# First turns and last turns of a gated linear-attention layer: W_out's high part by ScalarE, the scale-and-shift table in another PSUM bank, early z and h of the last group but one, and a residual added by TensorE

## The chip, the core and the metric

The kernel runs on one core of one Trainium2 chip. The metric is the time of one execution on the device in microseconds (us), the median of several. The engines are TensorE (PE in the profile; its weight loads are PEld), VectorE (DVE), ScalarE (ACT), GpSimd (POOL) and SyncE (SP), which here issues DMAs only. Each engine works through its own list of instructions in order and waits on semaphores that the others raise. SBUF is the working memory, PSUM the eight banks of 2 KB per partition into which TensorE writes; GpSimd cannot reach PSUM in this kernel's code, the others can.

## What is computed

`x` has 128 sequences of 64 rows of 256 numbers, in float32:

```python
xn = ln(x) * ln_w + ln_b
q = softmax((xn @ Wq + bq) in 8 heads of 32, over the 32)
k = softmax((xn @ Wk + bk - 1e6 * (1 - mask)) in 8 heads, over the 64 rows)
v = (xn @ Wv + bv) * mask
att = k^T v                      # per sequence and head, 32 x 32
y = q att                        # per sequence and head
scale, shift = split(silu(cond) @ W_emb + b_emb)
h = silu((ln(y) * ln2_w + ln2_b) * (1 + scale) + shift)
out = x + h @ W_out + b_out
```

Products are carried to near float32 accuracy as three products of rounded parts: with a = a_hi + a_lo and w = w_hi + w_lo, TensorE adds a_hi w_hi + a_hi w_lo + a_lo w_hi.

## The kernel before

The 8192 rows are cut into 16 groups of 512 rows (8 sequences, four tiles of 128 rows). A body function per engine, `body(i, ...)`, is one turn. Turns -1, 0, 1 and 2 are written out, turns 3 to 12 are a hardware loop of two turns per pass (on TensorE up to 14), the last turns are written out, and `tail()` ends each engine's list. The software pipeline has three stages: turn i does k, q and v of group i, attention and y of group i - 1, and layer norm of y, z, h and the output product of group i - 2. The last group, 15 (`L`), is worked in halves in the tail; group 14 is `M`. The order of each engine is the order of the code; nothing is scheduled by a tool.

For every group, x is brought in twice, as rows (`x_all`) and transposed (`xt_raw`). VectorE takes mean and variance per row (`x_stats`: `xstat`, `xmv`), GpSimd turns them into a scale and an offset per row (`x_rstd`: four small instructions on `xr`), VectorE turns these into rows (`x_rows`), SyncE writes them to DRAM with four small DMAs (`rows_stored`) and reads them back spread over all partitions (`rows_loaded`), and GpSimd applies them to `xt_raw` in four passes (`x_scaled`). ScalarE rounds the result to `xt_hi` (`x_high`), VectorE subtracts for `xt_lo` (`x_low`). `x_stats(g)` waits until `x_rstd(g - 1)` is done, since `xmv` has one buffer. Groups 0 and 1 go another way: their normed rows `xhat` are made directly, by ScalarE and GpSimd, and TensorE transposes them.

In turn i VectorE masks k and takes its maxima (`k_masked`, `k_max`), ScalarE takes exp(k) and copies it back after TensorE has transposed it (`exp_k_copied`), VectorE subtracts q's maxima (`q_max`, `q_shifted`), ScalarE takes exp(q), and after q's transposes it copies them (`q_copied`). `attention` and `y_product` on TensorE follow, with `kv_scaled` on VectorE between them. `y_sums` and `y_scaled_all` bring y out of PSUM, which frees the four banks `by`; `y_stats`, `y_scale` and `y_hat_all` are the second layer norm. In turn 0, VectorE's maxima of k have their own path: GpSimd subtracts them (`k_shifted`).

The banks: `by` is four banks. All four hold y between `y_product` and `y_scaled_all`. `be` names the first two, also used for the transposes of exp(k) and for attention; `bt` names the other two, also used for the transposes of q and for tanh(z). `bk` and `bv` are two banks each, for k, q and v and the output.

Three things are done once in turn 1: W_out is halved and split into `w_o_hi` and `w_o_lo` (`weights_o`, VectorE, lines 861 to 865), the condition's silu is finished (`silu_cond`), and TensorE makes the table of scale and shift (`emb_products`, line 1141) after the last q,v tile. It writes into bank `be[1]`, for which it waits until y of group 0 has been read, `ys_d`. ScalarE copies the table (`emb_copied`), and TensorE's second half of exp(k)'s transposes waits for that copy, because it writes the same bank.

In the tail TensorE adds residuals with an identity product: `x_added` starts the accumulation in the output's bank with x (plus bias, added by GpSimd in `x_biased`), and the output product goes on top. The result is then only copied. Groups up to 13 are added by VectorE (`residual`, line 1006) instead. The tail's `half_...` functions treat the two halves of group 15. SyncE stores group 14 when both halves' results of it are in `x_all`, and then group 15 in three pieces.

## Time and profile before

| | us |
|---|---|
| median of 3 runs | 306.88 (306.3 to 309.34) |
| the profiled execution's own time | 307.7 |
| its span, first to last instruction | 305.8 |
| TensorE busy | 291.8 (95%) |
| VectorE busy | 272.4 (89%) |
| GpSimd busy | 244.6 (80%) |
| ScalarE busy | 237.0 (77%) |

The granted clock of TensorE is 1.0 of full speed over the whole span. Matmuls overlap in the pipeline, and their ends are modelled, so what counts on TensorE is the start of one against the start of the next and the idle time that the profile names. In a timeline a row is: start, length, engine, line, operation, what it writes and reads, how many instructions are merged in it, and in brackets how long the engine stood idle before it and which instruction released it. Neighbouring instructions overlap by some 0.1 us, so a row's end lies a little behind the next row's start.

### The profile page before, as it was taken

What the parts mean: (1) busy time and instruction counts of PE and PEld (TensorE: products, weight loads), DVE (VectorE), ACT (ScalarE), POOL (GpSimd) and SP (SyncE); (2) the same over time, 40 slices, a digit from 0 to 9 for tenths busy, and PEclk for the clock granted to TensorE, in tenths of its full rate; (3) what the DMA queues carried; (4) which work ended last, traced back from release to release, by engine and by line L of the source; (5) the groups of instructions that cost most, each with busy time, mean ns of one, the idle gap of its engine ahead of it and who ended that gap; (6) DMA issues with size and microseconds to landing.
All of it is one profiled execution on the core that took longest, in us unless ns stands there. A gap on an engine that the chain in (4) does not pass through costs nothing.

```text
span 305.8 us, 14375 instructions
## 1 busy us (share of the span) xinstructions
PE 291.8 (95%) x5528; PEld 248.5 (81%) x5528; DVE 272.4 (89%) x640; ACT 237.0 (77%) x592; POOL 244.6 (80%) x246
## 2 busy tenths in 40 slices
PE   7999789899999999999999999999999999989875
PEld 7578588788989888988889898889888898877655
DVE  5899999989999999999999999999999796967793
ACT  1567758787978988898979888888989798776443
POOL 2275748989998989999998989898999979873470
PEclk9999999999999999999999999999999999999999
DMA  6983430704527080815325180906251341002024
GB/s 198 315 298 109 129 115 5 236 10 117 198 66 248 1 308 1 253 56 176 133 106 203 46 263 1 298 11 231 78 169 71 90 150 53 17 4 72 4 71 137
DMA packets 28445, 38.61 MB, mean 126 GB/s; under 512 B 2433, under 2 KB 20481, under 8 KB 28418
## 3 DMA queue, kind: packets, MB, share of 16 engines
q1 hardware_dynamic: 28000, 37.94, 38.1%
q8 instruction: 17, 0.28, 0.4%
q10 hardware_dynamic: 418, 0.30, 0.3%
q14 instruction: 10, 0.08, 0.1%
HBM read 29.80 MB, written 8.45 MB: 125 GB/s over the span
## 4 chain that ended last, share of the span: by engine, by line
PE 82%; DVE 9%; issue 4%; POOL 2%; DMA 1%; POOLq 1%; ACT 0%; SPq 0%; DVEq 0%
PE bk L1113 27%; PE bv L1113 27%; PE by L1113 15%; PE by L1198 4%; PE by L1177 4%; PE bv L1189 4%; DVE xstat L785 2%; DMA x_all<-in_x 1%; DVE k_t L909 1%; DVE q_s L898 1%; POOLq L45 1%; DVE qmax L890 1%; DVE th L843 1%; POOL xr L485 1%; DVE ystat L986 0%
## 5 line engine op out<-in xcount | busy, mean ns | idle before, releaser
L641 ACT ACTIVATE k_t<-k_t,kmax 128x64 f32<-128x64 f32 x240 | 60.5, 336 | 6.4 <-DVE kmax L916 6.2
L476 POOL TENSOR_TENSOR x_all<-x_all,bo_all 128x1024 f32 (+1 forms) x16 | 40.1, 2508 | 0.2
L436 POOL TENSOR_TENSOR h_lo<-h_s,h_hi 128x512 fp32r<-128x512 f32 x30 | 38.3, 1297 | 0.9 <-ACT h_hi L660 0.8
L445 POOL TENSOR_TENSOR xt_raw<-xt_raw,rows 128x512 f32<-128x512 f32 x28 | 37.0, 1322 | 1.5 <-DMA rows<-rows_dram 1.5
L447 POOL TENSOR_TENSOR xt_raw<-xt_raw,rows 128x512 f32<-128x512 f32 x28 | 36.5, 1303 | 2.2
L286 POOL TENSOR_TENSOR z_s<-z_s,mod_shift 128x512 f32<-128x512 f32 x30 | 30.7, 1044 | 6.8 <-DVE z_s L930 6.8
L595 ACT ACTIVATE y_s<-y_s,yr 128x256 f32<-128x256 f32 x56 | 29.1, 593 | 3.8 <-POOL yr L468 3.8
L1113 PE MATMUL bv<-w_o_hi,h_hi 128*128 128x256 f32 x120 | 31.6, 285 | 0.0
L1113 PE MATMUL bv<-w_o_lo,h_hi 128*128 128x256 f32 x120 | 31.0, 280 | 0.0
L580 ACT ACTIVATE v_s<-bk,small 128x256 f32<-128x256 f32 x32 | 15.1, 474 | 17.7 <-PE bk L1113 16.4
L1113 PEld LDWEIGHTS by<-kv,q_t 32*64 32x64 f32 x2048 | 22.4, 130 | 6.9 <-issue 6.5
L466 POOL TENSOR_TENSOR yr<-yr,neg_half 128x4 f32<-128x4 f32 x15 | 15.3, 1017 | 14.9 <-DVE yr L994 14.9
L1113 PE MATMUL bk<-xt_hi,w_k_hi 128*128 128x512 f32 x64 | 26.6, 416 | 0.3 <-ACT xt_hi L603 0.3
L580 ACT ACTIVATE v_s<-bv,small 128x256 f32<-128x256 f32 x32 | 15.2, 474 | 13.4 <-PE bv L1113 13.0
L1113 PE MATMUL bk<-xt_hi,w_k_lo 128*128 128x512 f32 x64 | 25.3, 395 | 0.0
L1113 PE MATMUL by<-kv,q_t 32*64 32x33 f32 x2048 | 24.4, 226 | 1.0 <-issue 1.0
L1113 PE MATMUL bv<-w_o_hi,h_lo 128*128 128x256 f32 x120 | 24.1, 282 | 0.2 <-POOL h_lo L436 0.2
L909 DVE SCALAR_TENSOR_TENSOR k_t<-off,bk 128x512 f32<-128x512 f32 x32 | 21.8, 680 | 2.1 <-PE bk L1113 1.7
L1113 PEld LDWEIGHTS bv<-w_o_hi,h_hi 128*128 128x128 f32 x120 | 22.6, 188 | 0.9 <-issue 0.2
L1113 PEld LDWEIGHTS bv<-w_o_lo,h_hi 128*128 128x128 f32 x120 | 22.6, 188 | 0.8 <-issue 0.2
L916 DVE TENSOR_REDUCE kmax<-k_t 128x8 f32<-128x512 f32 x32 | 21.8, 681 | 1.5
L454 POOL TENSOR_SCALAR xr<-xmv 128x4 f32<-128x4 f32 x15 | 14.3, 952 | 11.1 <-DVE xmv L789 9.9
(163 smaller groups left out, 865.9 us busy)
## 6 DMA issues: line engine op xcount, KB each, us to landing
x_all<-in_x SPq DMA_DIRECT2D x15, 512.0 KB, 6.4
out<-x_all SPq DMA_DIRECT2D x15, 512.0 KB, 5.0
xt_raw<-in_x_t SPq DMA_DIRECT2D x14, 512.0 KB, 6.1
rows<-rows_dram SPq DMA_DIRECT2D x14, 512.0 KB, 4.2
off<-in_mask_rows SPq DMA_DIRECT2D x16, 256.0 KB, 6.1
rows_dram<-xr_rows SPq DMA_DIRECT2D x56, 1.0 KB
x_all<-in_x SPq DMA_DIRECT2D x2, 256.0 KB, 3.5
z_s<-in_w_emb SPq DMA_DIRECT2D x1, 512.0 KB, 7.2
```

The costliest lines, as they stand in the source:

```text
L286: return eng.tensor_tensor(z, z, mod_shift[:, c, span(g, GB)].unsqueeze(2).broadcast_to([P, GB, SEQ]), ALU.add)
L436: nc.gpsimd.tensor_tensor(h_lo[:, c, :], h_s[:, c, :], h_hi[:, c, :].bitcast(fp32), ALU.subtract).then_inc(hlo_d, 1)
L445: nc.gpsimd.tensor_tensor(xc, xc, rows[:, parity, 0, :], ALU.mult).then_inc(xm_d, 1)
L447: nc.gpsimd.tensor_tensor(xc, xc, rows[:, parity, 1, :], ALU.add).then_inc(xs_d, 1)
L466: nc.gpsimd.tensor_tensor(yr[:, 1, :], yr[:, 0, :], neg_half[:, :], ALU.pow).then_inc(yr_d, 1)
L476: nc.gpsimd.tensor_tensor(xg, xg, bo_all[:, :].unsqueeze(1).broadcast_to([P, T, D]), ALU.add).then_inc(xb_d, 1)
L580: nc.scalar.activation(v_s[:, par, t, :, 0:DH], bqv[t][:, D:2 * D].rearrange("p (h d) -> p h d", d=DH), ACT.Copy, scale=mask_c[:, i * T + ...
L595: nc.scalar.activation(y_s[:, t, :], y_s[:, t, :], ACT.Identity, scale=yr[:, 1, t:t + 1], bias=yr[:, 3, t:t + 1]).then_inc(yhat_d, 1)
L641: last = nc.scalar.activation(kk, kk, ACT.Exp, scale=-1.0, bias=kmax[:, c, n:n + 1])
L909: nc.vector.scalar_tensor_tensor(k_t[:, par, c, :], off[:, par, :], sign, bk_[c][:, :], ALU.mult, op).then_inc(kadd_d, 1)
L916: nc.vector.tensor_reduce(out=kmax[:, c, :], in_=k_t[:, par, c, :].rearrange("p (b s) -> p b s", s=SEQ), axis=AX.X, op=ALU.max if first(i) ...
L1113: return nc.tensor.matmul(dst, lhsT, rhs, start=start, stop=stop)
```

## The change

The change has two parts.

**First two turns.** W_out is no longer halved in place. ScalarE writes the rounded half of it, `w_o_hi`, in turn 0, with scale 0.5 in the copy, between the first and the second v tile; VectorE makes `w_o_lo` in turn 1 in one instruction, 0.5 W_out - w_o_hi. Two of the four `xhat` tiles of group 1 go from ScalarE to GpSimd. In turn 0, VectorE takes q's maxima and differences ahead of and in the middle of the statistics of group 2; `x_rows(2)` goes from before `x_low(1)` to the end of the turn. GpSimd adds the bias to group 0's rows before `x_rstd(2)` instead of after it. In turn 1, VectorE scales y of group 0 before it shifts q of group 1. The table of scale and shift goes to bank `bt[1]`, the fourth of `by`, and the wait for its copy goes from the transposes of exp(k) to the second half of the transposes of q.

**End.** z of group 14 is scaled before the residual of group 13, and the first half of h of group 14 is made before y of group 15 is read. Its high and low parts get buffers of their own: the tiles of `w_qv_hi` and `w_qv_lo`, free after the last q,v tile. ScalarE makes the two high parts apart, GpSimd the two low parts apart, the first of them before the last group's `y_rstd`. The residual of group 13's second half is no longer added by VectorE: TensorE starts that bank with an identity product, and ScalarE copies the result. TensorE takes `x_added` of group 14's second half ahead of the last transposes of y.

```diff
+        h_hi_m = w_qv_hi
+        h_lo_m = w_qv_lo
...
@@ GpSimd, body, turn -1
                     x_rstd(1)
+                    pool.wait_ge(xt_d, 2)
+                    pool.wait_ge(xr_d, 8)
+                    for t in (2, 3):
+                        nc.gpsimd.tensor_scalar(xhat[:, t, :], x_all[:, 1, t * D:t * D + D], xr[:, 0, t:t + 1],
+                                                xr[:, 1, t:t + 1], ALU.mult, ALU.add).then_inc(xhat_d, 1)
...
@@ GpSimd, body
                 if first(i):
                     k_shifted(0)
                     k_shifted(1)
+                    x_biased(0)
                     x_rstd(2)
...
@@ GpSimd, end
+            def late_low(c):
+
+                pool.wait_ge(hhi_d, 2 * M + c + 1)
+                nc.gpsimd.tensor_tensor(h_lo_m[:, c, :], h_s[:, c, :], h_hi_m[:, c, :].bitcast(fp32),
+                                        ALU.subtract).then_inc(hlo_d, 1)
+
             def tail():
                 shifts(M)
+                late_low(0)
                 y_rstd(0)
                 y_half_hat(0)
                 y_rstd(1)
                 y_half_hat(1)
-                h_low(M, 0)
-                h_low(M, 1)
+                late_low(1)
...
@@ ScalarE
+            def weights_o_high():
+
+                act.wait_ge(wo_in, 16)
+                nc.scalar.activation(w_o_hi[:, :, :], w_o, ACT.Copy, scale=0.5).then_inc(wo_high, 1)
...
-                for t in range(T):
+                for t in (0, 1):
                     nc.scalar.activation(xhat[:, t, :], x_all[:, 1, t * D:t * D + D], ACT.Identity,
...
-                    nc.scalar.activation(emb[:, j, :], be[1][:, j * BATCH:(j + 1) * BATCH], ACT.Identity,
+                    nc.scalar.activation(emb[:, j, :], bt[1][:, j * BATCH:(j + 1) * BATCH], ACT.Identity,
...
                     v_tile(0, 0, 0)
+                    weights_o_high()
                     v_tile(0, 0, 1)
                     x_hat_one()
+                    v_tile(0, 0, 2)
                     k_exp_first(0)
-                    v_tile(0, 0, 2)
                     v_tile(0, 0, 3)
...
+            def late_high(c):
+
+                act.wait_ge(qv_d, 4 * L + 4)
+                act.wait_ge(h_d, 2 * M + c + 1)
+                nc.scalar.activation(h_hi_m[:, c, :], h_s[:, c, :], ACT.Copy).then_inc(hhi_d, 1)
...
                 z_tanh(M, th_of)
+                late_high(0)
+                result_out(L - 2, 1, bv_, o_d, 2 * (L - 2) + 2, res_d)
                 act.wait_ge(yr_d, 2 * L + 2)
                 y_hat(0)
-                h_high(M, 0)
-                h_high(M, 1)
+                late_high(1)
...
@@ VectorE
-            def weights_o():
-
-                dve.wait_ge(wo_in, 16)
-                link(nc.vector.tensor_scalar(w_o, w_o, 0.5, None, ALU.mult))
-                split(w_o, w_o_hi, w_o_lo)
+            def weights_o_low():
+
+                dve.wait_ge(wo_high, 1)
+                nc.vector.scalar_tensor_tensor(w_o_lo[:, :, :], w_o, 0.5, w_o_hi[:, :, :].bitcast(fp32),
+                                               ALU.mult, ALU.subtract).then_inc(weights_ready, 1)
...
                 if first(i):
-                    x_stats(2, 0)
-                elif not (isinstance(i, int) and i + 2 >= G):
+                    q_max(0, 0)
+                    q_shifted(0, 0, 0)
+                    x_variances(2, 0, (0, 1, 2))
+                    q_max(0, 1)
+                    q_shifted(0, 0, 1)
+                    x_variances(2, 0, (3,))
+                    x_means(2)
+                    x_low(1, by[:, 2:4, :])
+                    x_stats(3, 1)
+                    x_rows(2)
+                    return
+                if not (isinstance(i, int) and i + 2 >= G):
                     x_rows(i + 2)
...
-                if B:
-                    y_sums(i - 1)
-                q_shifted(i, par, 0)
-                if B:
+                y_sums(i - 1)
+                if second(i):
+                    y_scaled_all(0)
+                    q_shifted(1, 1, 0)
+                else:
+                    q_shifted(i, par, 0)
                     y_scaled_all(i - 1)
...
             def tail():
                 kv_scaled(L)
+                z_scaled(M)
                 residual(L - 2, 0)
-                z_scaled(M)
+                h_product(M, 0, th_of)
                 y_sums(L)
...
-                h_product(M, 0, th_of)
                 h_product(M, 1, th_of)
                 half_z(0)
-                residual(L - 2, 1)
                 half_z(1)
...
@@ TensorE
-                        last = mm(be[1][:, j * BATCH:(j + 1) * BATCH], w_e[c // 2][:, c % 2, j * P:(j + 1) * P],
+                        last = mm(bt[1][:, j * BATCH:(j + 1) * BATCH], w_e[c // 2][:, c % 2, j * P:(j + 1) * P],
...
                 for e in range(2):
-                    if second(g) and e == 1:
-                        pe.wait_ge(emb_out, 2 * C)
                     wait(pe, ys_d, 2 * (g - 1) + 2)
...
                 for c in range(C):
                     wait(pe, ys_d, 2 * g)
+                    if second(g) and c == 1:
+                        pe.wait_ge(emb_out, 2 * C)
...
                 pe.wait_ge(qsub_d, 4 * L + 2)
-                out_product(L - 2, 1)
                 pe.wait_ge(xb_d, G)
+                x_added(L - 2, 1, bv_)
+                out_tiles(bv_[1], h_hi, h_lo, 1, None, False).then_inc(o_d, 1)
...
-                pe.wait_ge(res_d, 2 * (L - 2) + 1)
+                pe.wait_ge(res_d, 2 * (L - 2) + 2)
                 x_added(M, 0, bv_)
+                x_added(M, 1, bv_)
                 half_y_transposed(1)
-                pe.wait_ge(res_d, 2 * (L - 2) + 2)
-                x_added(M, 1, bv_)
-                out_product(M, 0)
-                out_product(M, 1)
+                late_out(0)
+                late_out(1)
```

Three places show the order in the lists. A row is the line, the operation, what it writes and reads, and the semaphores that it waits for. First, VectorE in turn 0 from the end of k's maxima (`kmax`) to the first mask of turn 1; `xstat` and `xmv` are the statistics, `xt_lo` is group 1's low part, `xr_rows` is `x_rows`. Before:

```order
L916 TENSOR_REDUCE kmax<-k_t 128x8 [waits kadd_d]
L785 BN_STATS xstat<-x_all 128x6 [waits xr_d,x_in0]
L785 BN_STATS xstat<-x_all 128x6 x3
L789 BN_AGGR xmv<-xstat 128x2 [waits xstat_d] x4
L890 TENSOR_REDUCE qmax<-bv 128x16 [waits v_d]
L898 TENSOR_TENSOR q_s<-bv,qmax 128x512 [waits qmax_d]
L890 TENSOR_REDUCE qmax<-bk 128x16 [waits v_d]
L898 TENSOR_TENSOR q_s<-bk,qmax 128x512 [waits qmax_d]
L795 STREAM_TRANSPOSE xr_rows<-xr 128x32 [waits xr_d]
L923 TENSOR_TENSOR xt_lo<-by,xt_hi 128x1024 [waits hi_d]
L785 BN_STATS xstat<-x_all 128x6 [waits xr_d,x_in1]
```

And in the changed kernel:

```order
L926 TENSOR_REDUCE qmax<-bv 128x16 [waits v_d]
L934 TENSOR_TENSOR q_s<-bv,qmax 128x512 [waits qmax_d]
L818 BN_STATS xstat<-x_all 128x6 [waits xr_d,x_in0]
L818 BN_STATS xstat<-x_all 128x6 x2
L926 TENSOR_REDUCE qmax<-bk 128x16 [waits v_d]
L934 TENSOR_TENSOR q_s<-bk,qmax 128x512 [waits qmax_d]
L818 BN_STATS xstat<-x_all 128x6 [waits xr_d,x_in0]
L825 BN_AGGR xmv<-xstat 128x2 [waits xstat_d] x4
L959 TENSOR_TENSOR xt_lo<-by,xt_hi 128x1024 [waits hi_d]
L818 BN_STATS xstat<-x_all 128x6 [waits xr_d,x_in1]
L818 BN_STATS xstat<-x_all 128x6 x3
L831 STREAM_TRANSPOSE xr_rows<-xr 128x32 [waits xr_d]
```

The means of group 2 now come after q, and `xr_rows` has moved behind the statistics of group 3, which wait for `xr_d` of group 2.

Second, GpSimd in turn 0, from the end of `x_rstd(1)`; `k_t` is `k_shifted`, `x_all` is `x_biased(0)`, and the four `xr` rows after it are `x_rstd(2)`. Before:

```order
L425 TENSOR_TENSOR k_t<-k_t,kmax 128x512 [waits kmax_d] x2
L454 TENSOR_SCALAR xr<-xmv 128x4 [waits xmv_d,xhat_d]
L456 TENSOR_TENSOR xr<-xr,neg_half 128x4 [waits xr_d]
L458 TENSOR_TENSOR xr<-xmv,xr 128x4 [waits xr_d]
L460 TENSOR_SCALAR xr<-xr 128x4 [waits xr_d]
L476 TENSOR_TENSOR x_all<-x_all,bo_all 128x1024 [waits xstat_d,xhat_d,bo_in]
```

And in the changed kernel:

```order
L497 TENSOR_SCALAR xhat<-x_all,xr 128x256 [waits xr_d,xt_d]
L497 TENSOR_SCALAR xhat<-x_all,xr 128x256
L428 TENSOR_TENSOR k_t<-k_t,kmax 128x512 [waits kmax_d] x2
L479 TENSOR_TENSOR x_all<-x_all,bo_all 128x1024 [waits xstat_d,xhat_d,bo_in]
L457 TENSOR_SCALAR xr<-xmv 128x4 [waits xmv_d,xhat_d]
L459 TENSOR_TENSOR xr<-xr,neg_half 128x4 [waits xr_d]
L461 TENSOR_TENSOR xr<-xmv,xr 128x4 [waits xr_d]
L463 TENSOR_SCALAR xr<-xr 128x4 [waits xr_d]
```

Two `xhat` tiles stand ahead of `k_shifted`, and `x_biased(0)` stands ahead of `x_rstd(2)`.

Third, VectorE in the tail, from `kv_scaled` of group 15 to the first statistics of its y; `z_s` is z of group 14, `h_s` its h, `rq` is `y_sums`. Before:

```order
L947 TENSOR_TENSOR kv<-by,rk 128x4x66
L1006 TENSOR_TENSOR x_all<-bv,x_all 128x512 [waits o_d,xb_d]
L930 TENSOR_TENSOR z_s<-bk,mod_scale 128x512 [waits h_d,yt_d] x2
L966 RECIPROCAL rq<-by 128x32 [waits yr_d,y_d,ys_d,yt_d]
L977 TENSOR_TENSOR y_s<-by,rq 128x512 [waits rq_d]
```

And in the changed kernel:

```order
L983 TENSOR_TENSOR kv<-by,rk 128x4x66
L966 TENSOR_TENSOR z_s<-bk,mod_scale 128x512 [waits h_d,yt_d] x2
L1042 TENSOR_TENSOR x_all<-bv,x_all 128x512 [waits o_d,xb_d]
L991 SCALAR_TENSOR_TENSOR h_s<-th,z_s 128x512 [waits hlo_d,th_d]
L1002 RECIPROCAL rq<-by 128x32 [waits yr_d,y_d,ys_d,yt_d]
L1013 TENSOR_TENSOR y_s<-by,rq 128x512 [waits rq_d]
```

The residual has changed places with z, and one product of h stands ahead of `y_sums`.

## Rows read from the trace of the kernel before

**Rows 1.** Stretch of the loop: length, busy time (instructions) per engine, clock, DMA share, GB/s.

```profile
60.70:263.38 202.68, 202.68 (x4082) 176.15 (x4081) 187.69 (x439) 174.41 (x444) 186.45 (x175) 1.00 0.39 127
```

**Rows 2.** Timeline of TensorE in turns 1 and 2: start, length, instruction [idle <-releaser].

```profile
31.66 1.49 PE L1113 MATMUL by<-kv,q_t 32*64 32x33 f32 x128
...
38.11 0.68 PE L1113 MATMUL by<-th,z_s 128*128 128x128 f32 x4 [1.97 <-DVE y_s L971]
...
43.15 0.66 PE L1177 MATMUL by<-ident,k_t 128*128 128x128 f32 x4 [0.79 <-ACT emb L617]
...
47.32 1.04 PE L1198 MATMUL by<-ident,q_s 128*128 128x128 f32 x8
```

**Rows 3.** Timeline of VectorE in turns 0 and 1.

```profile
23.45 0.20 DVE L795 STREAM_TRANSPOSE xr_rows<-xr 128x32 f32<-128x32 f32 x1
...
24.69 1.40 DVE L785 BATCH_NORM_STATS2 xstat<-x_all 128x6 f32<-128x256 f32 x4
...
29.95 0.42 DVE L864 TENSOR_SCALAR y_s<-y_s 128x512 f32<-128x512 f32 x1
...
33.41 1.78 DVE L843 SCALAR_TENSOR_TENSOR th<-th 128x512 f32<-128x512 f32 x1
...
36.75 1.21 DVE L971 TENSOR_TENSOR y_s<-by,rq 128x1024 f32<-128x1024 f32 x1
```

**Rows 4.** Instructions of line 816: ns min/median/max, first and last start in us.

```profile
L816 DVE TENSOR_TENSOR w_k_lo<-y_s,w_k_hi x1: 692/692/692, 10.6 to 10.6; 128x512 fp32r<-128x512 f32 x1
L816 DVE TENSOR_TENSOR w_o_lo<-y_s,w_o_hi x1: 1640/1640/1640, 31.8 to 31.8; 128x512 fp32r<-128x512 f32 x1
```

**Rows 5.** Timeline of ScalarE in turns 1 and 2.

```profile
29.62 1.06 ACT L648 ACTIVATE q_t<-by 128x512 f32<-128x512 f32 x2
...
36.56 1.14 ACT L589 ACTIVATE xt_hi<-xt_raw 128x512 fp32r<-128x512 f32 x2
...
41.96 1.14 ACT L617 ACTIVATE emb<-by,small 128x128 f32<-128x128 f32 x4 [3.23 <-PE by L1113]
...
45.42 0.64 ACT L634 ACTIVATE q_s<-q_s 128x512 f32<-128x512 f32 x1
```

**Rows 6.** Timeline of GpSimd in turns 0 and 1.

```profile
20.93 0.19 POOL L454 TENSOR_SCALAR xr<-xmv 128x4 f32<-128x4 f32 x1 [0.33 <-DVE xmv L789]
...
22.73 2.40 POOL L476 TENSOR_TENSOR x_all<-x_all,bo_all 128x1024 f32<-128x1024 f32 x1
...
29.95 1.57 POOL L445 TENSOR_TENSOR xt_raw<-xt_raw,rows 128x512 f32<-128x512 f32 x1 [1.54 <-DMA rows<-rows_dram]
```

**Rows 7.** Instructions on the tiles `xr` and `rows`: ns min/median/max; DMA in us.

```profile
L454 POOL TENSOR_SCALAR xr<-xmv x15: 193/1177/1181, 16.7 to 230.0; 128x4 f32<-128x4 f32 x15
L488 POOL TENSOR_SCALAR xhat<-x_all,xr x2: 554/554/555, 9.2 to 9.8; 128x256 f32<-128x256 f32 x2
...
L445 POOL TENSOR_TENSOR xt_raw<-xt_raw,rows x28: 1286/1297/1740, 30.0 to 258.9; 128x512 f32<-128x512 f32 x28
...
DMA to landing us min/median/max: 3.8/4.2/5.0
```

**Rows 8.** Timelines of GpSimd, VectorE and TensorE in the tail.

```profile
285.75 2.04 POOL L286 TENSOR_TENSOR z_s<-z_s,mod_shift 128x512 f32<-128x512 f32 x2 [2.13 <-DVE z_s L930]
...
287.63 0.36 DVE L966 RECIPROCAL rq<-by 128x32 f32<-128x32 f32 x1 [1.37 <-PE by L1113]
...
300.24 0.69 DVE L1083 COPY x_all<-bv 128x512 f32<-128x512 f32 x1
...
291.83 0.66 PE L1332 MATMUL by<-ident,y_s 128*128 128x128 f32 x4 [1.85 <-POOL y_s L535]
...
293.19 1.02 PE L1113 MATMUL bv<-x_all,ident 128*128 128x512 f32 x2
```

**Rows 9.** Instructions of line 1064: ns min/median/max, first and last start in us.

```profile
L1064 DVE TENSOR_TENSOR q_s<-q_s,mod_shift x2: 784/1235/1686, 293.8 to 295.9; 128x512 f32<-128x512 f32 x2
```

**Rows 10.** One microsecond of the last stores, columns as in rows 1.

```profile
303.00:304.00 1.00, 0.00 (x0) 0.00 (x0) 0.00 (x0) 0.00 (x0) 0.00 (x0) 1.00 1.04 346
```

34 lines of the change are left out of this document (20 added, 14 removed).

## The prediction

> **What bounds the kernel now.** I read the stretches of the profile first, then the tensor engine in order of time with what ended its idle time, then the other engines in order of time around those gaps.
>
> From 60.70 to 263.38 TensorE is busy for 202.68 us of 202.68 [rows 1]: twelve turns at 16.89, no gap. VectorE has 187.69 of busy time there and GpSimd 186.45. So a turn costs what TensorE's work costs. Whatever TensorE gains before 60.7 is kept to the end of the loop; whatever another engine gains inside it is worth nothing. What can move is the opening and the tail.
>
> In the opening TensorE stands idle at two places [rows 2]. It waits 1.97 us before 38.11, for VectorE's `y_s` (line 971): the table products go to a bank that the scaled y of group 0 must leave first. And 0.79 us before 43.15, for ScalarE's copy of the table (line 617): the next transposes of exp(k) go to the table's bank. VectorE is why y is late. Ahead of it stand halving, rounding and subtracting W_out from 29.95 and the silu product that ends at 35.2 [rows 3].
>
> **The opening, step by step.** I take the times of before and shift them.
>
> *W_out.* VectorE loses the stretch 29.95 to 33.41, 3.46 us, and gets one subtraction back. Its price is not in the trace as such: 0.69 alone and 1.64 beside GpSimd are the same subtraction's two rows [rows 4]. I take 0.7, since GpSimd will be idle then (below). The silu product, 1.78 beside GpSimd [rows 3], I also take at 0.7, with 1.78 as the bound. ScalarE's rounding (about 0.6, as half of the 1.14 pair [rows 5]) I put at nothing: behind it two of ScalarE's four x_hat tiles leave for GpSimd, and the exp(k) after them waits for GpSimd. Without that cover it would cost its 0.6.
>
> *GpSimd in turn 0.* It takes two x_hat tiles at 0.55 [rows 7], and `k_shifted` comes 1.2 later, to 21.8. ScalarE's second exp(k) stood behind the last v tile until then anyway: no gain and no loss for TensorE's next transposes. Then comes `x_biased(0)`, moved ahead of the statistics of group 2: 2.40 [rows 6], to 24.2. The four steps of `x_rstd(2)` took 1.80, from 20.93 to 22.73; now they end at 26.0.
>
> *VectorE in turn 0.* The statistics of group 3 overwrite what `x_rstd(2)` reads, so they wait for it: 26.05 instead of 24.69 [rows 3], 1.36 late. `x_rows(2)` now stands behind them (0.13): masks, maxima and row exchange of turn 1 are 1.5 late. Queued behind on ScalarE are exp(k) and `q_copied`, which starts at 29.62 [rows 5] and ended at 30.68: now 32.17. TensorE's y product of group 0 needs it, so it starts at 32.25 instead of 31.66 [rows 2]: a new stall of 0.6. VectorE has by then done both short products (31.5 to 32.9). The y product ends at 33.7; reciprocal and scaling, 1.21 for the latter [rows 3] and now ahead of `q_shifted`, end at 35.5. TensorE's two q,v tiles end at 36.75, so the table products start there and not at 38.11: 1.37 gained. With the table in the fourth bank the 0.79 goes too, since the transposes of q that need this bank come 5 us later. TensorE alone would gain **2.16**.
>
> *The row exchange of group 2.* `x_rows(2)` moves from 23.45 to 27.65, and everything behind it with it. From its start to GpSimd's release by the DMA it took 6.50 [rows 3, 6]: now 34.15. (That is why GpSimd is idle beside the two short products.) GpSimd's four passes at 1.30 [rows 7] end at 39.45. ScalarE then does the second high part (0.57), the mask (0.6) and an exp(q) (0.6), less overlaps, to 41.1, and the table's copy; from there to the end of the next exp(q) it took 4.10, 41.96 to 46.06 [rows 5]: now 45.2. The transposes of q, at 47.32 [rows 2], can start at 45.25: **2.07**. Two chains of nearly one length, so I take 2.1. `x_rows(3)` must wait until the four small DMAs of group 2 have read their rows; they have 6.50 - 3.8 (the shortest landing of the large one [rows 7]) = 2.7 us, to 30.35, and with the shift of 1.5 `x_rows(3)` stands at 30.4: no stall, by a hair.
>
> **The tail.** Now the last turn's y is the path: `y_sums` at 287.63, then statistics, 291.83 on TensorE, the copy at 300.24 [rows 8], and before that the last shift at 295.9 [rows 9]. Four things change.
> - `h_product(M, 0)` goes ahead of `y_sums`. GpSimd's two shifts, from 285.75 on in 2.04 [rows 8], start some 0.25 sooner, since the residual no longer stands ahead of z, which then waits for its transposes. The first tanh ends at 286.55 + 0.65 = 287.2, while the second shift runs to 287.55. The subtraction that read two SBUF tiles beside GpSimd took 1.69 and alone 0.78 [rows 9], that is, it waited. So I let the product begin at 287.55 and end at 288.2: `y_sums` is **0.55 later**.
> - The residual of group 13's second half becomes an identity product, 1.02 for two passes [rows 8], in front of TensorE's idle 1.85 before 291.83: free, and ScalarE's copy of it falls where ScalarE waits for `yr`.
> - `x_added(M, 1)` goes ahead of the last y transposes. A pair of passes takes 0.85 to 1.02 [rows 8], and from 292.4 on stand transposes (0.5), two tiles (0.9) and now two pairs (1.75): the last transposes start at 295.5, **0.5** after their y is ready.
> - `late_low(0)` goes into GpSimd's idle time; `late_low(1)` ends at 295.9, before VectorE's last shift at 296.9, which so takes 0.78 and not 1.69: **0.9 won**.
>
> So the chain to the copy at 300.24 is 0.55 + 0.5 - 0.9 = 0.15 later, though the products of group 14 are done sooner. A last tile that came earlier would be hidden: the DMAs write the last 1.05 MB at 346 GB/s [rows 10], 3.0 us from the start of group 14's store, and that store waits for the copy. Tail: **0.15 lost**; bounds 0.4 gained (no late y) and 1.0 lost (no faster shift).
>
> By the Trainium skill ("SBUF — State Buffer", Who interferes with whom) a VectorE instruction with two SBUF inputs and a GpSimd instruction that reads SBUF exclude each other for the whole instruction. The rows agree: 1.64 and 1.69 beside GpSimd, 0.69 and 0.78 alone. By that rule the tail loses 0.15; were the two only to share, `y_sums` would be 0.25 late and the tail would gain 0.15.
>
> **Sum.** 2.1 - 0.15 = 1.95. The profiled execution took 307.7 for a span of 305.8; it would be 305.75 and the span 303.85. It lies 0.8 above the median of the runs, 306.88, so I forecast **304.9** for the median.
>
> **Rivals.**
> - *Everything idle is won.* If `x_rstd(2)` and `q_copied` come in time, TensorE gains 1.97 + 0.79, and 0.4 in the tail: 3.15, 303.7. Against it: the statistics' buffer makes VectorE wait, and ScalarE's chain allows 2.07.
> - *Half of it.* One link of the exchange is contended: the passes at 1.74, the longest, and not 1.30 would come 1.8 late [rows 7], two of them 0.9. That leaves 0.3 to 1.2: 305.8 to 306.7.
> - *GpSimd's chain takes the place of VectorE's.* All of `x_rstd(2)`, row exchange, passes, ScalarE, in series. First step 1.18, the median, and not 0.19: 1.0. Passes at 1.74: 1.8. Landing 5.0, the longest, and not 3.8: 1.2 [rows 7]. Together 4.0 against 2.1 won: 1.9 lost, and 0.15 in the tail, 308.9. It makes the kernel slower from 1.95 us of delay on. For it: the chain has no slack left where it had 2 us. Against it: the neighbours on VectorE in turn 0 read PSUM, and the DMAs are as free as before.
> - *The other bank lifts no wait*, because the fourth bank is taken sooner. Not so by the order: first user is the second half of q's transposes. It would cost 0.79: 305.7.
>
> Chances: forecast 0.60 (304.2 to 305.7), all idle time won 0.15, half 0.12, GpSimd's chain 0.07, the bank 0.03, something else 0.03. The range 303.4 to 306.4 leaves out GpSimd's chain and the far half of the second rival. About 1% is what a measurement tells from no change, here 3.07 us: faster than 303.8 has 0.17, the first rival and an edge of the forecast; slower than 309.9 has 0.03; same 0.80.
>
> **What would show it.** On VectorE a wait of about 1 us before group 3's first statistics, released by GpSimd's `xr`. On TensorE 0.5 to 0.7 idle before the y product of group 0, released by ScalarE, and none before the table products. GpSimd released by the rows' DMA near 34.1. Turns of 16.89 with the third starting near 58.6 instead of 60.7. In the tail `h_s` at 287.5 less 2.1, and the copy of group 14 no earlier than 298.2. I am wrong if turn 3 starts before 58.0 or after 59.5, or if the copy moves by more than 0.5 against it.

## The result, and the profile after

The changed kernel took **305.14 us**, the median of 21 runs (304.47 to 307.51). The kernel before, run beside it, took 309.02, also the median of 21 runs (306.3 to 311.67). The ratio of the two is 0.9939, with a 95% interval from 0.9917 to 0.9961, a gain of 1.9 us; it leaves out the runs that lie more than 1.5% above the fastest of their kernel, and so the longest of before, while the medians of all runs are 1.3% apart. The profiled execution took 304.73 us with a span of 302.9 (307.7 and 305.8 before). So the forecast of 304.9 us was met to 0.24 us, inside its range of 303.4 to 306.4. The gain, forecast as 1.95 us, was 1.9 by that ratio, but 2.9 between the profiled executions and 3.9 between the medians. The sections below are about these differences.

First the loop, a stretch between the same two instructions as [rows 1], with the same columns:

```profile
58.47:261.14 202.67, 202.67 (x4083) 176.09 (x4081) 188.29 (x439) 174.51 (x444) 187.03 (x177) 1.00 0.39 128
```

It lasts what it lasted before, 202.67 us, without idle time. It starts 2.23 us sooner, so all of the loop's part of the gain lies ahead of it.

The opening, TensorE's timeline (start, length, instruction, idle time before it and its releaser), to set beside [rows 2]:

```profile
32.72 1.48 PE L1156 MATMUL by<-kv,q_t 32*64 32x33 f32 x128 [0.87 <-ACT q_t L668]
...
37.03 0.61 PE L1156 MATMUL by<-th,z_s 128*128 128x128 f32 x4
...
40.60 1.04 PE L1218 MATMUL by<-ident,k_t 128*128 128x128 f32 x8
...
45.48 1.09 PE L1241 MATMUL by<-ident,q_s 128*128 128x128 f32 x8
...
52.99 0.50 PE L1156 MATMUL bk<-w_qv_hi,xt_hi 128*128 128x512 f32 x1 [0.35 <-issue]
```

VectorE beside it, to set beside [rows 3]:

```profile
26.49 1.40 DVE L818 BATCH_NORM_STATS2 xstat<-x_all 128x6 f32<-128x256 f32 x4 [1.12 <-POOL xr L463]
...
31.86 0.68 DVE L900 SCALAR_TENSOR_TENSOR w_o_lo<-y_s,w_o_hi 128x512 fp32r<-128x512 f32 x1
32.45 0.69 DVE L879 SCALAR_TENSOR_TENSOR th<-th 128x512 f32<-128x512 f32 x1
...
34.70 1.23 DVE L1007 TENSOR_TENSOR y_s<-by,rq 128x1024 f32<-128x1024 f32 x1
```

And GpSimd, whose row passes answer to [rows 6]:

```profile
34.48 1.29 POOL L448 TENSOR_TENSOR xt_raw<-xt_raw,rows 128x512 f32<-128x512 f32 x1 [4.22 <-DMA rows<-rows_dram]
```

The table products start without idle time, and the transposes of exp(k) of group 1 behind them too: both gaps of before are gone. There is a new gap of 0.87 us before the y product of group 0. The two short VectorE instructions take 0.7 us each, where the same silu product took 1.78: GpSimd is idle from 30.2 to 34.48, and its first pass now comes behind them.

The tail, by engine, to set beside [rows 8] and [rows 9]:

```profile
284.56 0.85 DVE L991 SCALAR_TENSOR_TENSOR h_s<-th,z_s 128x512 f32<-128x512 f32 x1 [0.63 <-ACT th L675]
285.33 0.34 DVE L1002 RECIPROCAL rq<-by 128x32 f32<-128x32 f32 x1
...
293.96 0.69 DVE L1108 TENSOR_TENSOR q_s<-q_s,mod_shift 128x512 f32<-128x512 f32 x1
...
297.35 0.68 DVE L1127 COPY x_all<-bv 128x512 f32<-128x512 f32 x1
...
299.34 0.42 DVE L1123 COPY x_all<-by 128x256 f32<-128x256 f32 x1 [1.30 <-PE by L1156]
```

```profile
289.52 0.66 PE L1382 MATMUL by<-ident,y_s 128*128 128x128 f32 x4 [1.46 <-POOL y_s L544]
...
292.60 0.60 PE L1382 MATMUL by<-ident,y_s 128*128 128x128 f32 x4
```

```profile
292.05 1.27 POOL L550 TENSOR_TENSOR w_qv_lo<-h_s,w_qv_hi 128x512 fp32r<-128x512 f32 x1
```

The first h product stands ahead of the sums of y. The last low part of GpSimd ends at 293.3, before VectorE's last shift at 293.96, which takes 0.69 us and not 1.69.

### The profile page after: what moved, and what is told of

The parts are those of the page before. It is cut to its first block, busy times and chain, and to the rows that moved or that the text cites. A ratio compares the mean times of both kernels' runs of the same rounds, so it can differ in the third digit from the quotient of the medians.

```text
span 302.9 us, 14378 instructions
## 1 busy us (share of the span) xinstructions
PE 291.5 (96%) x5530; PEld 248.2 (82%) x5530; DVE 267.8 (88%) x637; ACT 237.2 (78%) x592; POOL 244.5 (81%) x248
## 4 chain that ended last, share of the span: by engine, by line
PE 86%; DVE 4%; POOL 4%; issue 2%; DMA 1%; ACT 1%; SPq 0%; DVEq 0%; POOLq 0%
PE bk L1156 29%; PE bv L1156 28%; PE by L1156 15%; PE by L1241 4%; PE by L1218 4%; PE bv L1230 4%; DMA x_all<-in_x 1%; DVE xstat L818 1%; POOL x_all L479 1%; POOL xr L459 1%; ACT k_t L661 1%; POOL k_t L428 1%; POOL xr L488 1%; DVE w_qv_lo L893 0%; PE by L1382 0%
## 5 line engine op out<-in xcount | busy, mean ns | idle before, releaser
L448 POOL TENSOR_TENSOR xt_raw<-xt_raw,rows 128x512 f32<-128x512 f32 x28 | 36.3, 1298 | 4.2 <-DMA rows<-rows_dram 4.2
L450 POOL TENSOR_TENSOR xt_raw<-xt_raw,rows 128x512 f32<-128x512 f32 x28 | 36.1, 1290 | 2.2
L439 POOL TENSOR_TENSOR h_lo<-h_s,h_hi 128x512 fp32r<-128x512 f32 x28 | 35.4, 1287 | 0.5 <-ACT h_hi L680 0.4
L1156 PE MATMUL bv<-w_o_hi,h_hi 128*128 128x256 f32 x112 | 29.4, 284 | 0.0
L1156 PE MATMUL bv<-w_o_lo,h_hi 128*128 128x256 f32 x112 | 28.9, 280 | 0.0
L818 DVE BATCH_NORM_STATS2 xstat<-x_all 128x6 f32 (+1 forms) x64 | 22.6, 414 | 1.9 <-POOL xr L463 1.1
L1022 DVE BATCH_NORM_STATS2 ystat<-y_s 128x6 f32<-128x256 f32 x64 | 22.6, 414 | 0.5
L1156 PE MATMUL bv<-w_o_hi,h_lo 128*128 128x256 f32 x112 | 22.4, 281 | 0.0
L1156 PE MATMUL bk<-w_qv_hi,xt_hi 128*128 128x512 f32 x64 | 22.0, 422 | 0.4 <-issue 0.4
```

The lines of the kernel that those rows point to most:

```text
L439: nc.gpsimd.tensor_tensor(h_lo[:, c, :], h_s[:, c, :], h_hi[:, c, :].bitcast(fp32), ALU.subtract).then_inc(hlo_d, 1)
L448: nc.gpsimd.tensor_tensor(xc, xc, rows[:, parity, 0, :], ALU.mult).then_inc(xm_d, 1)
L450: nc.gpsimd.tensor_tensor(xc, xc, rows[:, parity, 1, :], ALU.add).then_inc(xs_d, 1)
L818: nc.vector.bn_stats(xstat[:, t, :], group_of(x_all, g)[:, :, t * D:t * D + D] .rearrange("p g n -> p (g n)")).then_inc(xstat_d, 1)
L1022: nc.vector.bn_stats(ystat[:, t, :], y_s[:, t, :]).then_inc(ystat_d, 1)
L1156: return nc.tensor.matmul(dst, lhsT, rhs, start=start, stop=stop)
```

## The experiments

Fourteen experiments (twelve new kernels, and a second profile of two), in four comparisons on four chips, each beside its own runs of the kernel before. They are told in the order of the argument. First one table for all of them. "Clock" is the mean granted clock of a run: 0.997 or more, or below 0.995. Times are medians in us; "idle" is TensorE's idle time in the profiled execution, before the y product of group 0 and before the table products. The changed kernel was not run beside any of them, so its row, and every comparison between chips, is good to half a microsecond at best: before itself, at 0.997 or more, has medians from 305.82 to 306.75 on the four chips.

| kernel | all runs | runs at 0.997 or more | runs below 0.995 | idle, y product / table |
|---|---|---|---|---|
| before, chip of front_only, tail_only, early_stats, early_stats_xadd | 308.96 | 10: 306.75 | 13: 310.27 | - |
| before, chip of before_warm, after_idle, wo_back, bank_back | 308.92 | 14: 306.05 | 15: 309.42 | - |
| before, chip of h_late, before_look, wo_back_look | 309.20 | 6: 305.82 | 11: 309.77 | 0 / 2.97 |
| before, chip of before_hold, hold_bank, hold_all | 309.08 | 8: 306.14 | 13: 310.19 | - |
| changed kernel | 305.14 | 16: 305.06 | 5: 307.17 | 0.87 / 0 |
| front_only | 306.30 | 7: 305.23 | 5: 306.92 | 0.86 / 0 |
| tail_only | 310.17 | 3: 306.16 | 9: 310.32 | 0 / 3.00 |
| early_stats | 304.59 | 6: 304.59 | 0 | 0 / 0 |
| early_stats_xadd | 303.94 | 5: 303.65 | 1: 305.01 | 0 / 0 |
| before_warm | 307.43 | 9: 307.06 | 3: 309.36 | 0 / 0 |
| after_idle | 310.25 | 0 | 6: 310.25 | 0.87 / 2.73 |
| wo_back | 305.99 | 6: 305.28 | 6: 307.26 | 0.87 / 0 |
| bank_back | 305.77 | 10: 305.64 | 2: 307.94 | 0.85 / 0 |
| h_late | 305.31 | 10: 305.17 | 2: 306.52 | 0.89 / 0 |
| before_hold | 304.91 | 12: 304.90 | 0 | 0 / 0 |
| hold_bank | 303.55 | 9: 303.43 | 1: 304.02 | 0 / 0 |
| hold_all | 303.58 | 6: 303.58 | 0 | 0 / 0 |

Two single runs, before_look with 308.47 and wo_back_look with 305.66, both at 0.997 or more, are not in the table.

### front_only and tail_only: which half of the change

front_only is the changed kernel with the old tail, tail_only the old opening with the new tail.

```diff
 front_only: the hunks of the change that touch turns -1 to 2
 tail_only:  the hunks that touch late_high, late_low, late_out, x_added(L - 2, 1), x_added(M, 1)
```

> The kernel before with the change of the first two turns alone; the end is as before. Theory (the opening carries the gain, 2.0 us between turn 1's y product and turn 3, the tail next to nothing): 1.9 to 2.1 us faster than before, ratio 0.9935; TensorE without a wait before the table products, 0.6 to 0.9 of idle before the y product of group 0, released by ScalarE. Rival (the tail is worth 0.9, the rest of the 2.9 us by which the two profiled spans differ): 1.2 to 1.5 us faster, ratio 0.996.

> The kernel before with the change of the end alone; the first two turns are as before. Theory: within 0.3 us of before, ratio 0.999 to 1.001: y of group 15 is read 0.4 to 0.55 later, the last transposes of y come 0.5 after their data, and the last shift takes 0.7 and not 1.69. Rival (the tail is worth 0.9): ratio 0.997.

front_only: 306.30, and 305.02 for the profiled run with a span of 303.2; ratio to before 0.9925 (0.9887 to 0.9964). Its opening is that of the changed kernel: 0.86 us before the y product, none before the table products, turn 3 from 58.91. So the opening carries the gain, and a tail worth 0.9 is out.

For the tail, count from the start of the last y product on TensorE to VectorE's copy of group 14. Inside that product some executions have an idle gap for which the profile names no releaser ("issue"): 0.54 us in before and in the changed kernel, 0.27 in front_only, none in several others. TensorE's rows of that product in the changed kernel, then product and copy in tail_only and in before_hold (below, with the old tail):

```profile
282.46 0.77 PE L1156 MATMUL by<-kv,q_t 32*64 32x33 f32 x55
283.77 0.98 PE L1156 MATMUL by<-kv,q_t 32*64 32x33 f32 x73 [0.54 <-issue]
```

```profile
288.98 1.74 PE L1127 MATMUL by<-kv,q_t 32*64 32x33 f32 x128
...
303.93 0.68 DVE L1098 COPY x_all<-bv 128x512 f32<-128x512 f32 x1
```

```profile
282.56 1.74 PE L1115 MATMUL by<-kv,q_t 32*64 32x33 f32 x128
...
297.04 0.68 DVE L1085 COPY x_all<-bv 128x512 f32<-128x512 f32 x1
```

| from the last y product to the copy, us | gap 0.54 | gap 0.27 or 0.28 | no gap |
|---|---|---|---|
| old tail | 15.04 (before), 15.03 (before_look) | 14.75 (front_only) | 14.48 (before_hold, hold_bank), 14.49 (before_warm) |
| new tail | 14.89 (changed kernel, bank_back, wo_back_look) | 14.89 (wo_back, early_stats), 14.90 (after_idle) | 14.95 (tail_only) |

The old tail takes 14.48 us and the gap, since `y_sums` waits for the product. The new tail takes 14.89 with or without it, since `y_sums` now stands behind the first h product and starts 2.87 us after the y product did, with a gap or without (2.93 in tail_only). So the new tail **gains 0.15 us where the gap is 0.54, and loses 0.14 where it is 0.27 and 0.4 to 0.5 where there is none**.

tail_only: 310.17; ratio 1.0049 (0.9998 to 1.01). By the medians this would be a tail that costs 1 us or more. Its profile says otherwise. TensorE in turn 1:

```profile
39.08 1.19 PE L1127 MATMUL by<-th,z_s 128*128 128x128 f32 x4 [3.00 <-DVE y_s L986]
...
45.17 0.61 PE L1127 MATMUL by<-th,h_s 128*128 128x128 f32 x4
```

Two of its microseconds, columns as for the loop, the seventh value is the granted clock:

```profile
41.00:42.00 1.00, 1.00 (x7) 1.00 (x7) 0.90 (x2) 0.00 (x0) 1.00 (x1) 0.50 0.03 12
45.00:46.00 1.00, 1.00 (x10) 0.98 (x9) 0.01 (x1) 0.18 (x1) 0.92 (x2) 0.92 0.00 0
```

In a stretch that the edit does not touch, the idle time before the table products is 3.00 us where it was 1.97 [rows 2], and behind it the granted clock is 0.50, the lower of TensorE's two levels (1.2 GHz), until 45 us; it was 0.66 in the last microsecond of the gap (38 to 39). The table products need 6.5 us instead of 3.65. So an execution of the old opening can be some 4 us longer than another, and the share of such runs decides its median.

### after_idle: does idle time before the table products bring the clock down?

```diff
 def emb_products():
-    pe.wait_ge(ys_d, 2)
+    pe.wait_ge(qsub_d, 8)
```

> The changed kernel, but the table products wait until VectorE has shifted the second half of q of turn 1 (about 39.9 us) instead of until y of group 0 has been scaled: TensorE then stands idle for some 2.85 us before them, where it now stands 0. Theory (an idle stretch of about 3 us lets the granted clock fall): in most runs the table products and what follows run at the lower level, the time grows by 2.85 + 2.9 = 5.7 us, to a median of 310 to 311, at most 2.85 in those where the clock stays. Rival (only the idle time itself counts): 2.85 us more, a median of 308.0, with the products at 3.6 us as now.

All six runs are below 0.995. The median is 310.25 against 305.14, 5.1 us more for a gap that is 2.73 us in the profiled execution. TensorE, and two microseconds of it:

```profile
39.50 1.20 PE L1156 MATMUL by<-th,z_s 128*128 128x128 f32 x4 [2.73 <-DVE q_s L934]
...
44.66 1.04 PE L1218 MATMUL by<-ident,k_t 128*128 128x128 f32 x8
```

```profile
41.00:42.00 1.00, 1.00 (x7) 1.00 (x7) 1.00 (x1) 0.00 (x0) 0.87 (x1) 0.50 0.82 308
42.00:43.00 1.00, 1.00 (x8) 1.00 (x8) 0.05 (x1) 0.00 (x0) 0.92 (x2) 0.67 0.07 28
```

The table products take 5.16 us (39.50 to 44.66) where they took 3.57 in the changed kernel. In this execution 2.73 idle and 1.6 at the lower clock make 4.3 of the 4.4 us by which it is longer than the changed kernel's. The theory's size was 1.3 us too large for this execution (it came from the one profile with 6.5 us), its sign and place right; the rival, 308.0, is out.

The Trainium skill ("TensorE: Matmul & The Clock Gate", HAM oscillation — how this bites in real kernels) tells of the same thing, a wait between products that makes the next ones start at the lower clock. The traces of tail_only and after_idle agree, at 3.00 and 2.73 us of idle time; before_look below, with 2.97 us, shows no such fall.

### before_warm: the old gap, filled with work

```diff
 def qv_tile(i, t):
+    if isinstance(i, int) and i == 1 and t == 3:
+        for _ in range(8):
+            mm(bqv[t][:, :], xt_hi[:, 0, tok], w_qv_hi[:, 0, :], True, True)
```

> The kernel before, with eight more 128x512 products of TensorE in turn 1 (at 0.23 us each, some 1.9 us) that write the bank of the last q,v tile before that tile itself is computed; they fill TensorE's idle time ahead of the table products (1.97 us in the profile of before, 3.00 us in that of the kernel with the change of the tail alone, where the granted clock was 0.50 from 40 to 45 us). Nothing else is changed, and the last tile has its 1.9 us to spare. Theory (the idle stretch is what lets the clock fall in many runs of before, and the fall costs some 2.9 us): the long runs of before, 308 to 312, vanish, the median is 306.5, between 306.0 and 307.0, 2 to 2.5 us under that of before in the same comparison, and no slice of the page shows a clock below 9 between 36 and 46 us. Rival 1 (the long runs of before have another cause): median and spread as before, 308.5 to 309.5. Rival 2 (the extra products delay what needs the tile): 308 or more with a new wait on ScalarE's v_s.

307.43 where before took 308.92 (ratio 1.0022, 0.9979 to 1.0065), above the 306.0 to 307.0 of the theory; 3 of 12 runs below 0.995 where before had 15 of 29. The gap is filled, the table products start at 37.84 and take 3.65. That is the theory's direction, but not its size: three of the long runs stay, and the runs at 0.997 or more are 1.0 us longer than those of before, 306.28 at the least against 304.57. The extra products fill a gap of 2 or 3 us, but where an execution of before had a shorter gap they may cost time (inferred, no such execution was profiled). With 12 runs this alone proves little. The table makes it plainer: with idle time before the table products (before, tail_only, after_idle) 67 of 108 runs are long ones by their clock; with the 0.87 us before the y product only (changed kernel, front_only, wo_back, bank_back, h_late) 20 of 69; with neither (early_stats, early_stats_xadd, before_hold, hold_bank, hold_all) 2 of 40. Where the clock falls in the 20 was not seen: no profiled execution is one of them.

### before_look: the kernel before a second time

No edit.

> The kernel before, unchanged, for a second profile of it. In about half of its runs the mean clock was 0.994 or less, and these took 308.5 us or more. Theory (the idle time ahead of the table products lets the clock fall): if this execution is one of those, the granted clock is 0.50 from about 39 us on, inside the table products, and these take 5 us or more instead of 3.6; the idle time ahead of them is 2 to 3 us. Rival (the fall lies elsewhere): in such an execution the table products take 3.6 us, and the low stretch is at another place. If the mean clock is 1.00, both expect 305 to 308 us.

It took 308.47, with a mean clock of 1.00 and a span of 306.7. VectorE, and then GpSimd and TensorE:

```profile
29.67 1.46 DVE L864 TENSOR_SCALAR y_s<-y_s 128x512 f32<-128x512 f32 x1
31.16 1.38 DVE L815 CAST w_o_hi<-y_s 128x512 fp32r<-128x512 f32 x1
32.58 1.65 DVE L816 TENSOR_TENSOR w_o_lo<-y_s,w_o_hi 128x512 fp32r<-128x512 f32 x1
34.15 1.77 DVE L843 SCALAR_TENSOR_TENSOR th<-th 128x512 f32<-128x512 f32 x1
```

```profile
29.55 1.29 POOL L445 TENSOR_TENSOR xt_raw<-xt_raw,rows 128x512 f32<-128x512 f32 x1 [1.42 <-DMA rows<-rows_dram]
```

```profile
38.85 0.68 PE L1113 MATMUL by<-th,z_s 128*128 128x128 f32 x4 [2.97 <-DVE y_s L971]
```

Here GpSimd's first pass starts at 29.55, 0.12 us *before* VectorE's halving of W_out, and the halving takes 1.46 us. In the first profile they started together, at 29.95, and it took 0.42 [rows 3, 6]. The pass is released by a DMA. Two more profiles of the old opening fit: in tail_only the pass was 0.09 us ahead (29.76 and 29.85) and the halving took 1.49, in before_warm 0.10 behind (29.78 and 29.68) and it took 0.42. So a DMA that lands some tenths sooner makes the gap 2.97 instead of 1.97. It also shows that a gap of 3 us does not bring the clock down every time.

### wo_back: W_out with VectorE again

```diff
 elif second(i):
-    weights_o_low()
+    weights_o()            # halve, round, subtract: three instructions on VectorE
 ...                        # and no weights_o_high() on ScalarE
```

> The changed kernel, but W_out is halved, rounded and subtracted by VectorE again, as before the change; all else stays. Reading of the trace so far: this work now falls where GpSimd is idle, at 0.42 and 0.69 instead of 1.41 and 1.64, so VectorE loses 1.1 us, while ScalarE is 0.6 us sooner with the copy of q that the y product of group 0 waits for (0.87 us in the profile after). The y product starts at 32.1, the table products wait 0.7 us and start where they start now, at 37.0 to 37.2: a time of 305.2, from 304.9 to 305.6. Rival (ScalarE's share is what won the 1.97 us, as the prediction costed it): the table products wait 1.5 us or more and start at 38, 306.2 or more.

In runs at 0.997 or more the median is 305.28, against 305.06 for the changed kernel on other chips. VectorE:

```profile
31.39 0.42 DVE L899 TENSOR_SCALAR y_s<-y_s 128x512 f32<-128x512 f32 x1
31.84 0.43 DVE L850 CAST w_o_hi<-y_s 128x512 fp32r<-128x512 f32 x1
32.31 0.69 DVE L851 TENSOR_TENSOR w_o_lo<-y_s,w_o_hi 128x512 fp32r<-128x512 f32 x1
32.92 0.68 DVE L878 SCALAR_TENSOR_TENSOR th<-th 128x512 f32<-128x512 f32 x1
```

All four take 2.2 us and not 5.2 or 6.3: GpSimd is idle beside them. The table products start at 36.57 with no idle time, 25.03 us behind turn 0's first product; in the changed kernel it is 25.02 (12.01 to 37.03). **In the profile, giving W_out to ScalarE won nothing**, and the medians differ by 0.2 us, less than chips do. Two numbers leave this weaker than it looks: against before on its own chip the ratio of wo_back is 0.9989 (0.9947 to 1.0032), and 6 of its 12 runs were below 0.995 where the changed kernel had 5 of 21. The counts are too small to say that the place of W_out changes how often the clock falls, or that it does not. The forecast of a gap of 0.7 was wrong too: the y product started no sooner, and VectorE had the 1.1 us to spare. A second execution, profiled to find where the clock falls in such a run, did not have the fall, and so did not tell:

> The changed kernel with W_out split by VectorE again, for a second profile. 6 of its 12 runs had a mean clock of 0.994 or less and took 306.4 to 308.4 us, though the profiled one shows no idle time ahead of the table products. If this execution is one of those: by the theory (idle time of TensorE in the opening lets the clock fall) the low stretch lies behind one of its idle gaps, that of 0.87 us before the y product of group 0 or a gap ahead of the table products that the other execution did not have. Rival: the low stretch has no idle gap before it, or lies in the tail. If the mean clock is 1.00: 304.6 to 305.6 us.

305.66 us, 0.85 us before the y product, nothing before the table products.

### before_hold: the kernel before with one wait more

```diff
 if N and c == 0 and not first(i):
+    if second(i):
+        pool.wait_ge(silu_c_ready, 1)
     x_scaled(i + 1, 1 - par, c)
```

> The kernel before with one wait more: in turn 1 GpSimd starts its four passes over the turned x of group 2 only when VectorE has done the silu product, that is, behind VectorE's work on W_out, where before it started by the landing of a DMA at 29.95 us (29.55 in a second profile) and lay beside it. Theory (the collision is the cause): VectorE's five instructions take 0.42, 0.43, 0.69 and 0.69 us, 2.2 in all instead of 5.2 to 6.2, y of group 0 is scaled by 35.5, the table products start behind the last q,v tile with no idle time, at 36.1; GpSimd's passes end at 37.2 instead of 36.2, which ScalarE has to spare. The time is 307.7 - 2.0 = 305.7 us at full clock, the median 305.3 to 306.0, without runs above 308; the fall of the clock is rare. Rival 1 (the work on W_out costs what it costs, the collision is small): 307 to 309 with a gap of 1.5 us or more. Rival 2 (the later passes delay the transposes of q): the gap is gone, but a new wait on ScalarE stands before the transposes of q near 46, and the time is 307 or more.

**304.91 us**, with not one run above 306.17, where before took 309.08 (ratio 0.9948, 0.9916 to 0.998). One wait does as much as the whole change (0.9939). It is 0.4 us less than the 305.3 to 306.0 that was expected. VectorE and GpSimd:

```profile
29.67 0.42 DVE L866 TENSOR_SCALAR y_s<-y_s 128x512 f32<-128x512 f32 x1
30.13 0.43 DVE L817 CAST w_o_hi<-y_s 128x512 fp32r<-128x512 f32 x1
30.59 0.69 DVE L818 TENSOR_TENSOR w_o_lo<-y_s,w_o_hi 128x512 fp32r<-128x512 f32 x1
31.20 0.68 DVE L845 SCALAR_TENSOR_TENSOR th<-th 128x512 f32<-128x512 f32 x1
```

```profile
31.97 1.27 POOL L445 TENSOR_TENSOR xt_raw<-xt_raw,rows 128x512 f32<-128x512 f32 x1 [3.83 <-DVE th L845]
```

GpSimd's passes start 2 us later and end 0.9 us later than in [rows 6], as the four take 5.25 us from start to end and not 6.39; VectorE's silu product ends 3.3 us sooner than in [rows 3]. The table products have no idle time before them, and ScalarE is done with x of group 2 before it is asked for the table. That the collision is the cause of the 1.97 us is shown: it alone was taken away, and the gap went.

By the Trainium skill ("SBUF — State Buffer", Who interferes with whom) the two engines share a port pair, a lock held for a whole instruction, and who issues first keeps it. The traces agree: 0.42 when VectorE's halving starts with the pass or ahead of it, 1.46 and 1.49 when the pass is 0.12 and 0.09 us ahead.

### bank_back and hold_bank: what the other bank is worth

```diff
 bank_back: after, emb_products and emb_copied on be[1], the wait for the copy at the transposes of exp(k)
 hold_bank: before_hold, emb_products and emb_copied on bt[1], the wait at the second half of q's transposes
```

> The changed kernel, but the table's products go to the second bank again, as before the change, so that the second half of the transposes of exp(k) of group 1 waits for ScalarE's copy of the table. The prediction has 0.79 us on this: the wait comes back before the second half of these transposes, near 42.0, with 0.7 to 0.8 us; the transposes of q depend on ScalarE's chain, which the bank does not touch, and stood only some 0.2 us behind TensorE's own order, so 0.6 to 0.8 us of it reach the end: 305.8, from 305.5 to 306.1. Rival (ScalarE's chain sets the transposes of q alone): within 0.2 us of the changed kernel, 305.2.

> The kernel before with the same wait of GpSimd, and with the table in the fourth bank as in the changed kernel; W_out stays with VectorE, and the opening keeps its order. Theory: both idle gaps of the opening are gone, without the 0.87 us before the y product of group 0 that the changed kernel has: 305.7 - 0.8 = 304.9 us, from 304.5 to 305.3, at least as good as the changed kernel's 305.14. Rival (ScalarE's chain of x of group 2, exp(q) and the table's copy sets the transposes of q): no better than with the wait alone, 305.5 or more.

bank_back: ratio 0.9973 (0.993 to 1.0016); 305.64 in runs at 0.997 or more, against 305.06 for the changed kernel on other chips; and the wait is back on TensorE:

```profile
41.70 0.66 PE L1220 MATMUL by<-ident,k_t 128*128 128x128 f32 x4 [0.94 <-ACT emb L637]
```

Of 0.94 us, 0.84 reach the transposes of q in the profile (13.60 us behind the y product, 12.76 in the changed kernel), and the medians differ by 0.6. In hold_bank the bank is worth more, 303.55 against 304.91 on one chip, 1.4 us, and more than expected (304.5 to 305.3). Between the two profiles the transposes of q start 1.0 us sooner, of which 0.8 is the wait (at 40.69 in before_hold); another 0.3 is an "issue" gap that was smaller in that execution (below). hold_bank is 1.6 us below the changed kernel, by medians from different chips; the ratios to before, 0.9882 and 0.9939, say the same.

### h_late, early_stats, early_stats_xadd, hold_all: the rest

```diff
 h_late:           after, h_product(M, 0) behind y_stats, late_high(0) and late_low(0) beside (1)
 early_stats:      after, group 2's statistics in one piece before q_max(0, 1), x_rows(2) before x_stats(3, 1),
                   x_rstd(2) before x_biased(0)
 early_stats_xadd: as that, x_added(M, 1) behind half_y_transposed(1)
 hold_all:         hold_bank with tail_only's tail, x_added(M, 1) behind half_y_transposed(1)
```

> The changed kernel, with the early z and h of group 14 undone: the first h product behind the statistics of the last y, both of ScalarE's high parts and both of GpSimd's low parts where they stood before the change; the own h buffers and the residual by TensorE stay. The prediction has two terms on this: the sums of the last y 0.55 us late (0.45 in the profiles with and without the change of the tail), and 0.9 us won at the last shift, which no low part of GpSimd then lies beside. Undone, the sums come 0.45 us sooner after the end of the last y product, the last shift takes 1.7 us instead of 0.7, and the copy of group 14, from which the last stores count, comes 0.1 to 0.5 us later: a time of 305.4, from 305.2 to 305.7, against 305.14. Rival (the early h is worth nothing or costs, since its lateness of the sums goes straight to the end): 304.7 to 305.0, with the last shift at 0.7.

305.31, within 0.2 us of the changed kernel, which between chips decides nothing. Counted from the start of the last y product, which has no gap here, the sums of y come 1.88 us behind it (2.87 in the changed kernel) and the copy of group 14 14.48 (14.89). The last shift takes 1.26 instead of 0.69, and TensorE waits for the low part:

```profile
294.14 0.51 PE L1156 MATMUL bv<-w_o_hi,w_qv_lo 128*128 128x256 f32 x2 [1.05 <-POOL w_qv_lo L550]
```

Both terms of the prediction are there: the lateness of `y_sums` is 0.99 where there is no gap, not 0.55, and the shift is 0.57 longer here. Which is larger depends on the gap, as in the table above.

> The changed kernel, but in turn 0 VectorE finishes the statistics of group 2 (fourth tile and means) before q's second maxima and writes x_rows(2) before the statistics of group 3, and GpSimd does x_rstd(2) before it adds the bias to group 0. Theory (the new stalls, 1.12 on VectorE before group 3's statistics and 0.87 on TensorE before the y product of group 0, come from x_rstd(2) behind the bias and the late means): both go, masks of turn 1 start 1.3 to 1.5 earlier, and the kernel is 0.7 to 0.9 us faster than the changed one, ratio to before 0.9905. Rival (ScalarE's chain or the contention of GpSimd's passes with VectorE's two short products of W_out and silu takes its place): under 0.3 us faster than the changed kernel, ratio 0.993.

> The same, and in the tail TensorE's x_added(M, 1) stands behind the last transposes of y again. Theory (the transposes waited 0.5 to 0.8 behind it, and what follows them to the copy of group 14 sets the end): the last transposes, the last shift and the copy come 0.6 to 0.8 earlier against y_sums, the kernel is 0.4 to 0.7 faster than early_stats, ratio 0.9885. Rival (TensorE's own products of groups 14 and 15 set the end): same as early_stats within 0.2 us.

early_stats: 304.59 (ratio 0.987, 0.9816 to 0.9925); the 0.87 us before the y product are gone (0.57 us of "issue" stand inside it), turn 3 starts at 57.67. early_stats_xadd: 303.94 (0.9856, 0.9801 to 0.9911). Its profiled opening was 0.5 us later, behind a load of W, and its copy of group 14 came 14.49 us behind the start of the last y product, against 14.89. So `x_added(M, 1)` ahead of the last transposes cost 0.4 us, near the prediction's 0.5. In both, GpSimd's first pass starts only just behind VectorE's silu product (31.26 and 30.84, 31.53 and 31.42), so here too a DMA decides who goes first, and ScalarE's share of W_out may be worth something; that was not tried.

> As the last one, with the change's tail (early z and h of group 14, own h buffers, the residual by TensorE), but the residual of the second half of group 14 behind the last y transposes. From runs so far the tail is worth 0.13 us and this last place 0.4: 304.9 - 0.5 = 304.4 us, from 303.8 to 304.9. Rival (the tail's parts are hidden by the last stores): 304.9, as without them.

303.58 (ratio 0.9894, 0.9846 to 0.9942): with hold_bank's opening the new tail adds nothing that can be told from 303.55, as the rival said, though not for its reason as far as is known. The new tail with the residual in its old place takes 14.49 us (with a gap of 0.54), and hold_bank's old tail 14.48 (with none). hold_bank and early_stats_xadd beat the two kernels of this case: hold_bank with a ratio of 0.9882 (0.9841 to 0.9922), early_stats_xadd with 0.9856, on different chips.

## Why the prediction was right, and where it was wrong

**The opening of the changed kernel: right, step by step.** VectorE's wait before group 3's statistics, 1.12 <-POOL xr, forecast 1. The passes released at 34.48, forecast 34.15. The y product at 32.72 with 0.87 idle, forecast 32.25 and 0.6; 0.1 of the lateness was there in turn 0 (12.01 against 11.89 for its first product). The table products at 37.03 without idle time, forecast 36.75. The transposes of q at 45.48 and not 45.25, turn 3 at 58.47 and not 58.6. Without the 0.1, one lateness of 0.3 runs through VectorE's steps: GpSimd's `x_rstd(2)` ended at 26.39 and not 26.0, group 3's statistics began at 26.49 and not 26.05, and the stall was mis-sized by 0.3. It did not reach the table products, since y was scaled by 35.93 and they wait for the q,v tiles.

**The cause: wrong.** The step that failed is "VectorE is why y is late. Ahead of it stand halving, rounding and subtracting W_out". The amount of VectorE's work was not the reason: with the silu product it is 2.2 us alone, and in wo_back's profile it stays on VectorE and the table products start no later. Of the term "VectorE loses the stretch 29.95 to 33.41, 3.46 us", 1.9 us were the collision: alone the three instructions take 1.54. GpSimd's row passes lay beside it and made 2.2 us into 5.2, or 6.3 when the passes came first (before_look). The prediction had the rows for it, 0.69 and 1.64, and used them to price the new order, but it did not ask what the old order would cost with the collision alone removed. The new order of turn 0 removed it as a by-product, by making the row exchange late; the same lateness made the new stall of 0.87. before_hold buys the gain without the stall.

**The size of the gain: wrong.** The second step that failed is the base: "It lies 0.8 above the median of the runs, 306.88". The sum of 1.95 was set against one execution as if before had one time, and the fall of the clock was put at nothing. The median of before came out at 309.02 and the gain between medians at 3.9. In 90 runs of before beside the experiments (38 with a clock of 0.997 or more, median 306.45, and 52 lower, median 309.8) the old opening spreads from 304.6 to 312.3. No rival spoke of the clock, and the median of three runs, 306.88, was a lucky one. That 304.9 lies 0.24 us from the measured median is luck in part: a base 2.1 us too low, and a gain between medians 1.9 too low. By the ratio the gain is 1.9, and between the medians of runs at 0.997 or more it is 1.4 (306.45, on other chips, and 305.06). The changed kernel wins, over the forecast, the executions in which the gap was 3 us and those in which the clock fell behind it. That a fall costs what it does is shown by after_idle; that most of the long runs of before fall at this gap is inferred from the counts, 67 of 108 against 2 of 40, and from tail_only's profile. That the shortest runs of before, 304.6 to 305.5, are those in which the passes came late enough by chance fits before_hold's 304.4 to 306.2, but no such execution was profiled.

**Between the two profiles,** 2.9 us: 2.0 from the opening, less 0.1 for its later start, 0.15 from the tail, 0.8 from smaller "issue" gaps on TensorE, idle time for which the profile names no releaser, and 0.1 not assigned. In before's execution they sum to 2.57 us, in after's to 1.76; in the other profiles to between 1.4 and 2.9, with no relation to the edit. They lie in the turns that are written out; in the loop there is one, of 0.22 us, in early_stats. That part of the 2.9 is no gain of the change.

**The tail: each term near, the sum wrong, and its sign set by a gap that the sum left out.** Forecast 0.15 lost. Between the two profiles, both with a gap of 0.54 us in the last y product, 0.15 was gained: `y_sums` is 0.44 late (forecast 0.55), the residual of group 13 is free, the last transposes come 3.08 after the first (forecast 3.1), and the last shift is 1.0 shorter (forecast 0.9). Each term is within 0.1, and their errors sum to 0.3. What the prediction did not see is that the gap was part of its 287.63: without it `y_sums` stood 0.54 sooner before the change and no sooner after it, so its lateness is 0.99 and the tail loses 0.4. The prediction had named a copy of group 14 before 298.2, or a move of more than 0.5 against turn 3, as a sign of error. The copy came at 297.35, and 0.66 sooner behind turn 3 than before: 0.4 of that is a smaller "issue" gap in front of the tail, 0.15 the tail, 0.1 not assigned. The h product began 0.3 before GpSimd's shift ended (282.82 and 2.04) and took 0.85, so it ended 0.1 sooner than the exclusion gave it.

**Rivals.** That everything idle is won did not happen; half of it, a GpSimd chain, a bank that lifts nothing did not either. GpSimd's row passes took 1.26 to 1.30 each, and the landing came as taken.

## What to carry to other kernels

When an instruction takes twice its usual time, take the collision away first and the instruction second: hold back the neighbour that has slack (here GpSimd, by one wait on a semaphore that exists) before work is moved to another engine. Where a DMA's landing decides who of two engines that exclude each other goes first, the kernel has several times and not one; a forecast then needs a profile of each, and the fix is worth most in the bad ones. The tail says the same: a gap that comes and goes on TensorE made one change gain 0.15 us or lose 0.4, so count from the same instruction in several profiles. An idle gap of 2 to 3 us on TensorE must be priced with the clock that may fall behind it, not only with its own length.

## What the runs showed of the hardware

- GpSimd's pass starting 0.09 or 0.12 us ahead, or else together or 0.10 us behind, decided between 1.46 to 1.49 and 0.42 us for one VectorE instruction with one input (`TENSOR_SCALAR`, 128x512 float32, SBUF to SBUF), and a `CAST` of that size took 0.43 alone and 1.38 to 1.41 beside GpSimd's passes.
- Idle gaps on TensorE of 3.00 and 2.73 us were followed by a granted clock of 0.50 for 6 and 3 us; one of 2.97 us and one of 1.97 us in other executions by none. In all 6 runs of the kernel in which such a gap was forced (2.73 us in the profiled one) the mean clock was below 0.995.
- Between executions of nearly the same kernel the unexplained "issue" gaps on TensorE varied from 1.4 to 2.9 us in sum, and the one inside the last y product was 0.54, 0.27 or absent. Their cause stays open; no run was made for it.
